# Gated cross-attention with a routed expert layer: four buffers for the probabilities, closing rooms over them, and new orders

## The reference

```python
x = x + tanh(g_xattn) * attention(layernorm(x), ctx, ctx)     # 16 heads of 32
x = x + tanh(g_ffn) * ffn(layernorm(x))

# attention: Q = ln @ Wq.T + bq, K and V = ctx @ W.T + b, scores = Q K^T / sqrt(32),
#            softmax over the 512 keys, times V, then @ Wo.T + bo
# ffn:       p = softmax(t @ router_w + router_b); idx = argmax(p); gate = max(p)
#            y = gate * (t @ expert_w[idx] + expert_b[idx])   # 8 experts of 512x512
```

## Time and profile before

| what | value |
|---|---|
| median of three runs | 1055.9 us (1054.35 to 1056.93) |
| profiled execution, its own time | 1057.68 us |
| its span | 1056.0 us |
| PE busy | 978.0 us, 93% |
| ACT busy | 811.9 us, 77% |
| DVE busy | 745.6 us, 71% |
| POOL busy | 262.0 us, 25% |
| mean granted TensorE clock | 0.976 |

### The profile page before, as it was taken

The page is one execution under the profiler, slowest core; times in us unless marked ns, Lnnn a source line. Parts: engine busy times, 40 slices in busy tenths (PEclk is TensorE's granted clock), DMA queues, the critical chain, the costliest instruction groups (busy, mean ns, idle before and its releaser), DMA issues.

```text
span 1056.0 us, 18686 instructions
## 1 busy us (share of the span) xinstructions
PE 978.0 (93%) x5208; PEld 641.8 (61%) x5208; DVE 745.6 (71%) x1653; ACT 811.9 (77%) x1913; POOL 262.0 (25%) x318
## 2 busy tenths in 40 slices
PE   3798999999999999999999999999999997698996
PEld 2564467656765676567656765676567545576775
DVE  5745655875787578757875787578757778797664
ACT  3688988898889888978898889888988988233431
POOL 6002200430042004200420042004201006454663
PEclk9799999999999999999999999999999989799999
DMA  6334223532443245324532453244325259144542
GB/s 213 97 90 114 79 64 98 143 85 69 115 137 89 69 110 140 89 60 117 136 81 70 117 137 84 68 116 137 86 69 132 62 166 378 56 135 137 163 138 75
DMA packets 70884, 119.37 MB, mean 113 GB/s; under 512 B 17854, under 2 KB 18878, under 8 KB 70656
## 3 DMA queue, kind: packets, MB, share of 16 engines
q1 hardware_dynamic: 64544, 99.49, 34.0%
q0 software_dynamic: 6240, 18.68, 5.5%
HBM read 50.42 MB, written 18.66 MB: 65 GB/s over the span
## 4 chain that ended last, share of the span: by engine, by line
PE 69%; ACT 10%; DVE 7%; issue 6%; DMA 3%; POOL 2%; SPq 2%; DVEq 1%; ACTq 0%; POOLq 0%
PE jb L489 11%; PE jb L490 10%; PE jb L491 10%; PE jb L532 10%; PE sc L512 9%; PE hb L522 9%; PE sc L673 6%; ACT jb L707 5%; ACT probs L695 3%; DVE maxima L819 1%; DVE e_lo L836 1%; PE hb L659 1%; PE jb L603 1%; SPq L452 1%; DMA q_stack<-q_lo 1%
## 5 line engine op out<-in xcount | busy, mean ns | idle before, releaser
L819 DVE TENSOR_REDUCE maxima<-jb 128x1 f32<-128x512 f32 x512 | 335.7, 686 | 112.0 <-PE jb L532 109.5
L707 ACT ACTIVATE jb<-jb,maxima 128x512 f32<-128x512 f32 x512 | 341.9, 678 | 41.4 <-DVE maxima L819 38.0
L695 ACT ACTIVATE probs<-sc 128x512 f32<-128x512 f32 x512 | 284.4, 605 | 40.7 <-PE sc L512 29.2
L532 PE MATMUL jb<-k_stack,q_stack 96*128 96x512 f32 x512 | 207.6, 434 | 24.4 <-ACT jb L707 10.1
L512 PE MATMUL sc<-q_stack,k_stack 98*128 98x512 f32 x512 | 183.9, 423 | 2.8 <-ACT probs L695 1.8
L532 PEld LDWEIGHTS jb<-k_stack,q_stack 96*128 96x128 f32 x512 | 95.9, 191 | 109.1 <-ACT jb L707 59.1
L522 PE MATMUL hb<-probs,values 128*32 128x512 f32 x1024 | 138.8, 616 | 1.0 <-ACT probs L695 0.7
L512 PEld LDWEIGHTS sc<-q_stack,k_stack 98*128 98x128 f32 x512 | 94.1, 191 | 67.9 <-ACT probs L695 36.6
L707 ACT ACTIVATION_READ_ACCUMULATOR jb<-jb,maxima 128x1 f32 x512 | 113.2, 221 | 0.0
L1104 POOL TENSOR_TENSOR stage<-stage,gbo 128x512 f32<-128x512 f32 x31 | 39.8, 1284 | 253.8 <-DMA stage<-in_x 253.8
L1096 POOL TENSOR_TENSOR row<-rt,tiny 128x2 f32<-128x2 f32 x15 | 12.7, 848 | 259.5 <-DVE rt L901 259.5
(11 more groups left out here) (228 smaller groups left out, 1740.3 us busy)
## 6 DMA issues: line engine op xcount, KB each, us to landing
k_stack<-k_hi SPq DMA_DIRECT2D x256, 64.0 KB, 2.0
q_stack<-q_hi SPq DMA_DIRECT2D x256, 64.0 KB, 2.0
stage<-in_x SPq DMA_DIRECT2D x63, 256.0 KB, 3.0
...
k_stack<-k_lo SPq DMA_DIRECT2D x128, 64.0 KB, 2.0
q_stack<-q_lo SPq DMA_DIRECT2D x128, 64.0 KB, 2.0
e_lo<-in_ew SPq DMA_DIRECT2D x8, 1024.0 KB, 10.8
...
```

Source lines behind the costliest of these rows:

```text
L532: nc.tensor.matmul(jbs[j][:], q_stack[g % 2][0:MAXROW, n * P:(n + 1) * P], k_stack[g % 2][0:MAXROW, h * S:(h + 1) * S], start=True, stop=T ...
L695: nc.scalar.activation(probs[:, kt % 2, h, :], scs[(16 * g + n) % NSC][:], ACT.Exp)\
L707: nc.scalar.activation(jbs[j][:], jbs[j][:], ACT.Exp, bias=maxima[g % 2][:, n:n + 1], accum_out=row_sums[g % 2][:, n:n + 1]).then_inc(s["m ...
L819: nc.vector.tensor_reduce(maxima[g % 2][:, n:n + 1], jbs[j][:], AX.X, ALU.max, negate=True)\
```

## The change

1. `probs` gets four buffers, one for each key tile. E of tile kt now waits for the product of the same tile in the group before.
2. `late_room`, `done_room` and `late_spots` are laid over the third and fourth buffer. The value weights are loaded into the third buffer at the opening, so E of tile 2 waits for three weights to be split, not two. The last x tile is loaded only when all products P are done.
3. The scratch for descriptors of dynamic DMAs halves.
4. The four order tables and the bank table are written anew for every engine.

```diff
-        probs = sb("probs", [P, 2, HG, S])
-        late_room = sb("late_room", [P, HG * S])
-        done_room = sb("done_room", [P, S])
-        late_spots = sb("late_spots", [P, S])
+        probs = sb("probs", [P, NT, HG, S])
...
+        late_room = kept("late_room", [P, HG * S])
+        done_room = kept("done_room", [P, S])
+        late_spots = kept("late_spots", [P, S])
...
-        nat = [probs[:, 0], probs[:, 1], late_room[:, :].rearrange("p (c o) -> p c o", o=S), values[:, :, :]]
+        nat = [probs[:, 0], probs[:, 1], probs[:, 2], values[:, :, :]]
...
                 if (kind, t, n) == ("DR", B - 1, NT - 1):
-                    wait(sp, s["w_lo_done"], 4 * NF)
+                    wait(sp, s["pv_done"], NT * NG * B)
...
-                            probs[:, n % 2, h, :], start=(n == 0), stop=(n == NT - 1))
+                            probs[:, n, h, :], start=(n == 0), stop=(n == NT - 1))
...
-                    wait(act, s["w_lo_done"], 2 * NF)
-                    wait(act, s["pv_done"], NT * g + kt - 1)
-                    nc.scalar.activation(probs[:, kt % 2, h, :], scs[(16 * g + n) % NSC][:], ACT.Exp)\
+                    wait(act, s["w_lo_done"], (3 if kt == 2 else 2) * NF)
+                    wait(act, s["pv_done"], NT * (g - 1) + kt + 1)
+                    nc.scalar.activation(probs[:, kt, h, :], scs[(16 * g + n) % NSC][:], ACT.Exp)\
...
-    nc = bacc.Bacc("TRN2", target_bir_lowering=False, num_devices=1, dynamic_dma_scratch_size=8192)
+    nc = bacc.Bacc("TRN2", target_bir_lowering=False, num_devices=1, dynamic_dma_scratch_size=4096)
```

A line of a table, SP in the closing:

```diff
-        "~DR2 W3 W0 ~~RW3 W1 W6 ~~RW2 ~DR1 ~DR3 W2 W4 W5 W7 EB ~RW0 ~RW1 ~RW3 ~RW2",
+        "~DR1 W0 W2 W6 W1 ~~RW2 ~~RW3 W3 ~DR2 W4 ~DR3 W5 W7 EB ~RW0 ~RW1 ~RW2 ~RW3",
```

More of the change, by code:

```diff
@@ L34 @@
     "SP": [
-        "1SQ0 1SK0 1SK1 1SQ1 ~~RW2 ~~RW3 1SQ2 1SQ3 1SK2 1SK3 ^DC0 2SQ0 2SQ1 2SK0 2SQ3 2SK2 1MD 2SQ2 2SK1 2SK3 ^DC1 ~RW0 ^DC2",
-        "^DC3 ~RW1 3SK0 ~DR2 3SQ0 ~DR3 ^DX0 3SK1 ^DX1 2MD 3SQ1 ^DX2 3SQ2 ^DX3 3SK2 3SQ3 3SK3 DR0 3MD ^0SQ0 ^0SQ1 ^0SK0 ^0SK1",
-        "^0SQ2 ^0SK2 ^0SQ3 ^0SK3 ^0MD DR1",
+        "~~RW3 1SK0 1SQ0 1SQ1 ~~RW2 1SK1 1SQ2 1SQ3 1SK2 1SK3 2SQ0 ^DC0 2SQ1 2SQ2 2SK0 2SQ3 1MD 2SK3 2SK2 2SK1 ^DC1 ^DC2 ^DC3",
+        "~RW0 3SQ0 ~DR2 3SK0 3SK1 ~DR3 ^DX0 ~RW1 ^DX1 2MD 3SQ1 3SK2 ^DX2 3SQ2 ^DX3 3SK3 3SQ3 DR1 DR0 3MD ^0SQ0 ^0SQ1 ^0SK0",
+        "^0SK1 ^0SK2 ^0SQ2 ^0SQ3 ^0SK3 ^0MD",
     ],
     "PE": [
[10 rows of a table removed]
[10 rows of a table added]
     ],
     "ACT": [
[8 rows of a table removed]
[8 rows of a table added]
     ],
     "DVE": [
[5 rows of a table removed]
[5 rows of a table added]
     ],
     "POOL": [
-        "C3 ~~OP2 ~~OP3 LX0 LX1 LX2 LX3 ~OP0 ~~LR1 ~OP1 ~LR0 ^C0 ^C1 ^C2",
+        "C3 ~~OP2 ~~OP3 LX0 LX1 LX2 LX3 ~OP0 ~OP1 ~~LR1 ~LR0 ^C0 ^C1 ^C2",
     ],
@@ L74 @@
     "SP": [
-        "^DC0 ^DC1 ^DC2 LW1 LC ^DC3 ^DX0 LW0 ^DX1 ^DX2 LW2 ^DX3 ^0SK1 ^0SK0 LW3 ^0SK3 ^0SK2 ^0SQ0 ^0SQ1 ^0SQ2 ^0SQ3 ^0MD",
+        "^DC0 ^DC1 ^DC2 LW1 LC ^DC3 ^DX0 ^DX1 LW0 ^DX2 ^DX3 LW2 LW3 ^0SK0 ^0SK3 ^0SK2 ^0SK1 ^0SQ0 ^0SQ1 ^0SQ3 ^0SQ2 ^0MD",
     ],
     "PE": [
[4 rows of a table removed]
[4 rows of a table added]
     ],
     "ACT": [
[4 rows of a table removed]
[4 rows of a table added]
     ],
     "DVE": [
[3 rows of a table removed]
[3 rows of a table added]
     ],
@@ L100 @@
     "SP": [
-        "1SQ1 1SK0 1SQ0 1SQ3 1SK1 ~~RW3 1SQ2 ~~RW2 ~DR2 1SK2 1SK3 ~DR3 2SQ0 2SQ1 2SK0 2SK2 2SK1 DR0 2SK3 1MD 2SQ2 2SQ3 3SK0",
-        "3SQ0 3SQ1 3SQ2 2MD 3SK1 ~RW1 ~RW0 3SQ3 3SK2 3SK3 3MD",
+        "~~RW3 1SK0 1SQ0 ~DR3 ~~RW2 1SQ3 1SK1 1SQ1 1SK3 1SQ2 1SK2 2SQ0 2SK0 2SQ1 2SK1 2SK3 2SQ2 1MD 2SK2 ~DR2 2SQ3 3SK0 3SQ0",
+        "3SK1 3SQ1 ~RW0 2MD 3SQ2 ~RW1 DR0 3SK3 3SK2 3SQ3 3MD",
     ],
     "PE": [
[6 rows of a table removed]
[6 rows of a table added]
     ],
     "ACT": [
[5 rows of a table removed]
[5 rows of a table added]
     ],
     "DVE": [
[3 rows of a table removed]
[3 rows of a table added]
     ],
     "POOL": [
-        "C3 ~~OP2 ~~OP3 LX0 LX1 LX2 LX3 ~~LR1 ~OP0 ~OP1 ~OP2 ~LR0 ~OP3",
+        "C3 ~~OP2 ~~OP3 LX0 LX1 LX2 LX3 ~OP0 ~OP1 ~~LR1 ~LR0 ~OP2 ~OP3",
     ],
@@ L160 @@
 BANK_TABLE = [
-    "012310231031031031201203120103210320301301",
-    "3201321301203102310231023102031201230120310213023012012012012301201231301201202013213",
-    "21032021031031231201320132013213210021032023102310213201303210310310310321031032021023023020231031",
-    "03210203213213010320132013201301302230213231023120321302101320120120120132012013032031031030312012",
-    "01320301321321020130213021302102103310321312031230132103202130230230230213023021013012012010123023",
-    "02130102132132032012301230123023021102130103210312013021323012312312312301231230201203203202031231",
-    "23012023013013213203120312031231230023012021302103201230131203103103103120310312320321321323210310",
-    "31203231201201301321032103210310312231203230123021320312010321021021021032102103132130130131302102",
-    "10321310320320320321021302132132132121231012301230130123",
-    "012302012310230",
+    "012310231031031031021021021312031203201301",
+    "3021301320320132013201320132013201320132101302132013013013012301301302012301202013203",
+    "21031010231021021032130213021021023123120312031210302310213210310310310231031031212013203101032102",
+    "13023030123013013021320132013013012312310231023130201230132130230230230123023023131032102303021301",
+    "32012020312032032013210321032032031231230123012302123102301302102102102310210210303201321020213023",
+    "01231212031201201230132013201201203103102310231012320312013012312312312031231231010213023121230120",
+    "13203232103213213201302130213213210310312031203132021032130132032032032103203203131230120323201321",
+    "30210202310230230213012301230230231031032103120310203210312310210210210321021021313012302101023103",
+    "12032013213201302312130132013201322121213203120312031203",
+    "120310130201320",
 ]
```

## The result

The change makes the kernel slower. Its median is 1068.3 us in 4 runs (1065.3 to 1072.2); in the same job the kernel before took 1056.4 us. The ratio is 1.0116, with a 95% interval of [1.0078, 1.0154]. The forecast was 1048.6 us. The profiled execution took 1065.3 us, the one of before 1057.7, so the two traces differ by 7.6 us.

A forecast was written before the change was run, and what follows sets the result against it. It took PE to pace the batches and chains of latency the opening and closing. Its terms, -1.2 - 4.8 - 1.0 + 1.0 + 1.2 - 2.5 = -7.3 us, gave 1050.4 against the profiled execution, 1048.6 us as median; range 1041 to 1058.5.

The forecast's parts named there:

- The closing: Closing, up to Y0: fewer gathers ahead of W4 on POOL let W4 start near 890.5 to 891; -2.5 us (-6 to +3).
- It moves with W4: Closing: Y0 comes about 9 us after W4's start plus 4.5, as before, so Y0 shifts with W4.
- Rival B: Closing: W2 behind LR0 on DVE waits 4.5 us for W4, Y0 comes +2.7; 1053.8 us, no change; chance 0.09.
- The banks: Batches 1 to 6: PE waits less for PSUM banks to return; -0.8 us a batch, -4.8 us in all.
- ACT rarely waited for a P: Batches: ACT waited ahead of an E about 1 us a batch with 12 to spare, so E's freedom by itself gains nothing.
- My own sign of being wrong: Middle batches: the forecast is wrong if they stay at 105 us or more; 103 to 105 were expected.
- The pair of products: Batches 1 to 6: joining one pair of products P on PE saves about 0.2 us a batch; -1.2 us in all.
- Batch 0, batch 7, opening: Bank waits fall in batch 0 (-1.0 us) and rise in batch 7 (+1.0); later statistics delay the opening, +1.2 us (0 to +3).
- The wait of E by itself: Batches: E no longer waits for P two tiles back; by itself nothing, it lets the lists place P later.
- the scratch: POOL's gathers and scatters: at most some five are under way, so the halved ring costs nothing.
- C: Batches: waits change places, the banks' term is 0 and batch 7 costs 2; sum -1.5, 1054.4 us; chance 0.12.
- A: Middle batches: ACT late, RT2 waits 1.4 us or more, some 0.8 us a batch lost; 1059.4 us; chance 0.14.

The follow-up runs named there:

- b_closing_new: The kernel before with the change's new closing lists of all five engines and their banks, old memory and scratch; ratio 1.0081 to the kernel before.
- a_rt2_later: The changed kernel with RT2 moved behind scores S4 and S5 on PE in the middle batches; ratio 1.0094 to the kernel before.
- b_rooms_only: The kernel before with the change's four buffers, rooms, waits and half the scratch, but lists and bank digits of before; ratio 1.0025 to the kernel before.
- b_scratch_half: The kernel before with only the scratch for dynamic DMAs halved, 8192 to 4096; ratio 1.0027 to the kernel before, 1.0011 when repeated.

## Why the prediction was wrong

**The closing: -2.5 forecast, +7.8 in the profiles, about +8.5 by b_closing_new.** The step that failed is "I take **-2.5 us** (-6 to +3)" as the term of the whole closing. It was worked out for the 30 us up to Y0 and put at nothing, without a reason, for the 135 us from Y0 to Y38, with new lists on PE, ACT, DVE and POOL. Those 135 us became 145.6. "It moves with W4" held: W4 started 1.4 us sooner (892.03 instead of 893.46) and Y0 1.1 us sooner. The part that I did cost was right in kind and too large, for W4 was to start at 890.5 to 891. Of what was lost behind Y0, the runs show one place, Y20 to Y26 with POOL's order (3.0 us here). The losses from Y0 to Y6 (+2.0), Y14 to Y20 (+1.0) and Y32 to Y38 (+1.9) no run takes up; their causes stay open. Expert weights and PE in the changed kernel, answering to the earlier trace rows:

```profile
892.03 4.53 POOL L1107 TENSOR_TENSOR e_lo<-e_lo,e_hi 128x2048 fp32r<-128x2048 f32 x1
...
892.89 5.83 DVE L836 TENSOR_TENSOR e_lo<-e_lo,e_hi 128x2048 fp32r<-128x2048 f32 x1
...
899.25 7.01 DVE L836 TENSOR_TENSOR e_lo<-e_lo,e_hi 128x2048 fp32r<-128x2048 f32 x1
...
899.59 4.52 POOL L1107 TENSOR_TENSOR e_lo<-e_lo,e_hi 128x2048 fp32r<-128x2048 f32 x1
907.01 1.09 PE L659 MATMUL hb<-ident,tiles_room 128*128 128x128 f32 x4 [5.48 <-DVE heads_lo L1042]
908.19 0.79 PE L673 MATMUL sc<-e_hi,heads_hi 128*128 x1
```

W3 runs once W4 is done, and W7 is held up by W5. Rival B's place, W2 behind LR0, did not decide: W2 was done ahead of W4.

**The banks: -4.8 forecast, about +4.5 for batches 1 to 6 with the pairs of products in it.** The step that failed is "I take -0.8 us a batch for the banks". My count named the new wait (RT2, 0.5 to 1 us) and its size rightly. It failed in taking the short places apart from each other: RT2's waits took back all that M6's gave (4.2 us each), and in a_rt2_later a bank with more room shortened nothing, for ACT paced that stretch. "ACT rarely waited for a P", and so E's freedom was put at nothing; that P would wait for E, 1.4 to 2.0 us in six batches, had no place in the count, nor had the waits for `xn_lo` and for DMAs other than M0's. The one wait that I said stays, M0's, is the one that shrank (4.5 to 1.6 us). My own sign of being wrong, batches of 105 us or more, came: 633.7 / 6 is 105.6.

**The pair of products: -1.2 forecast.** The pair takes 1.85 to 1.86 us in all six batches, as in the earlier trace rows. The pair costs what I said; whether it saved the 0.2 us can't be seen beside +1.9 us behind P as a whole.

**Batch 0, batch 7, opening: -1.0, +1.0, +1.2 forecast.** Averages of all profiles, 4 with the new lists (a_rt2_later among them) and 13 with the old: batch 0 102.5 against 102.7, batch 7 68.0 against 69.5, opening 75.6 against 76.4. Batch 0 is unchanged, and batch 7 and the opening are small gains, within the scatter or near it, where I had forecast losses: both signs were wrong. In the opening the steps came as followed through: CS ended at 13.96 (13.95 forecast), LX0 ran at 14.70 (14.9), POOL took it up at 15.93 (16.0). Yet Q0 started at 28.06, against 28.08 in the earlier trace rows:

```profile
15.93 0.96 POOL L1086 TENSOR_TENSOR rt<-rt,tiny 128x1 f32<-128x1 f32 x1 [2.54 <-DVE rt L854]
...
28.06 0.74 PE L489 MATMUL jb<-xn_hi,wq_hi 128*128 128x512 f32 x1 [1.82 <-DVE xn_lo L858]
```

The 2.2 us by which POOL was late were made up before Q0, where I had let 0.4 to 1.3 of them through.

**The wait of E by itself and the scratch: nothing forecast, nothing found.** b_rooms_only is at 1.0025 [1.0006, 1.0045], and its batches 1 to 6 take 629.9 us, as in the other profiles with the old lists. With b_scratch_half first at 1.0027 and then at 1.0011, I can't call its 0.25% a cost.

**The rivals.** None was it. C had the batches' mechanism, waits that change places, but at no cost. A named the slower end for the batches (+0.8 a batch, measured +0.75) but by ACT's lateness at RT2, and RT2's wait was 0.7 and not 1.4. The chance of 0.16 for slower was too small: no rival, either, put a loss behind Y0.
